# Two fused layers on one core: VectorE's first step on a gate tile moved next to its second step

## The chip, the cores and the metric

The kernel runs on one core of one Trainium2 chip. The metric is the device time of one execution in microseconds (us); the time of a version is the median of its runs. TensorE (PE in the rows) multiplies, its weight loads are PEld; VectorE is DVE, ScalarE is ACT, GpSimd is POOL, and SyncE (SP) issues most transfers.

## The reference

Two transformer layers on 2048 tokens of width 256, each of the form `x + attention(layernorm(x)) + ffn(layernorm(x))`. The first layer has linear attention and an FFN with ternary weights, and this FFN is where the change lies:

```python
def _L0_ffn_ref(x, W_up, W_gate, W_down):
    wu = ternary_quant(W_up)
    wg = ternary_quant(W_gate)
    wd = ternary_quant(W_down)
    up = jnp.einsum('bsd,ed->bse', x, wu)
    gate = jnp.einsum('bsd,ed->bse', x, wg)
    hidden = jax.nn.silu(up) * gate
    return jnp.einsum('bse,de->bsd', hidden, wd)
...
xn = _layernorm(x, axis=-1)
x = x + _L0_attn_ref(xn, ...) + _L0_ffn_ref(xn, ...)
xn = _layernorm(x, axis=-1)
x = x + _L1_attn_ref(xn, ...) + _L1_ffn_ref(xn, ...)
```

The second layer has softmax attention with rotary positions and an FFN with Hadamard-rotated weights.

## The kernel before, in words

`work_order()` writes one list of pieces (`gate`, `up`, `down`, `kv_in`, `att_n` and so on). Each engine walks this same list and, for every piece whose name it has a function for, issues its own instructions of that piece. So the list fixes the order of each engine's queue; engines meet only at semaphores. An engine that waits in one piece holds back everything behind it in its own queue.

The first layer's FFN goes over four chunks c of 512 tokens and, in each, over eight tiles m of 128 hidden units; f = 8c + m numbers them, and `gate 2` below means the gate piece of f = 2. TensorE forms the activated product in `gate` (line 938, four matmuls with the weights TU) and the other one in `up` (line 951, four with TG). Three tiles later `down` (line 917, weights TD) adds the tile's share of the output. Between these pieces `weave` puts pieces of the first layer's attention (`kv_in`, `kv_sum`, `att_n`, `att_t`, `att_b`, `q0`) and of the preparation of weights (`tern_cut`, `scales`, `spread_vb`, `butterfly`).

For the first two chunks (c below WHOLE = 2) silu is built from tanh, since exp of the attention is in the same table as tanh. The chain of one tile f is:

- TensorE `gate` writes a PSUM bank; ScalarE writes tanh of half of it to the buffer sg (line 1495, semaphore t);
- VectorE's first step: sg = (sg + 1) times the gate bank (line 1258, semaphore v1). This reads the gate bank for the last time;
- TensorE `up` writes another bank; VectorE's second step: sg = sg times the up bank (line 1267, semaphore h);
- ScalarE copies sg to hh (line 1503), GpSimd makes the rest hl (line 1633), and TensorE's `down` takes both.

From the third chunk on ScalarE applies Silu itself, and there is no first step on VectorE.

The gate and up products take their PSUM banks from one ring of three, banks 3, 4 and 5, in the order gate, up, gate, up. So `up` of tile f + 1 gets the bank of `gate` of tile f and waits, before its first matmul, for that tile's v1 (line 941); `gate` of tile f + 2 gets the bank of `up` of tile f and waits for h. The side pieces have banks 0 and 1: `att_n` (line 849) waits for the bank that the last `att_n` or `kv_in` left, which VectorE frees at line 1238 (`at`, the attention output divided by its sum) or line 1207.

VectorE's side pieces in the stretch at issue: `tern_cut` (line 1177) makes the ternary weights TD, 1024 columns at a time; `kv_in` is lines 1206 and 1207; `kv_sum` line 1226; `scales` lines 1193 to 1197; `spread_vb` line 1181; `att_n` lines 1232, 1234 and 1238; `att_t` line 1245; `att_b` line 1250.

Of the kernel before, what the change touches and what calls it, by code (L numbers as in the profile page):

```python
# [8 lines left out]
ALU = mybir.AluOpType  # L9
# [12 lines left out]
WHOLE = 2  # L22
# [422 lines left out]
def program(nc, x_d, wa0, tern, wa1, wo1, wf1, cols_d, bkv_d, cos_d, sin_d, had_d, mask_d, ident_d, pad_d, sel_d, wl_d, ob_d, wsd_d, y_d):  # L445
    with ExitStack() as ctx:
        base = -(-nc.sbuf_base // 32) * 32

        def sb(name, kb, shape, dt=F32):
            return nc.alloc_sbuf_tensor_at(name, shape, dt, offset=base + int(kb * KB))  # L450

        q = {n: ctx.enter_context(nc.semaphore(f"s_{n}")) for n in SEMAPHORES}
# [46 lines left out]
        sg = [sb(f"sg{i}", 168 + 2 * i, [128, 512]) for i in range(3)]  # L499
# [37 lines left out]
        bank = [PS[:, i, :] for i in range(8)]  # L537
# [56 lines left out]
        def way_out(e, p):  # L594
            (s_o, n_o), (s_n, _), (s_r, _), _ = o_slots(p)
            i, o = p // 4 % 2, p % 2
            e.dma_start(scr_o[p].rearrange("c k n -> (c k) n"), OE[o][:, :]).then_inc(d[s_o], 16)
            e.wait_ge(d[s_o], n_o)
            if p > 1:
                t, n = o_slots(p - 2)[3]  # L600
                e.wait_ge(d[t], n)
            e.dma_start(RC[o][:, :], scr_o[p, :, 16, :].rearrange("c (q n) -> c q n", n=16)).then_inc(d[s_r], 16)
            if p > 7:
                e.wait_ge(q["gl"], p // 4 - 1)
            for h in range(2):
                row = 32 * (p % 4) + 16 * h
                e.dma_start(NUM[i][row:row + 16, :].rearrange("r (a n) -> r a n", a=2),
                            scr_o[p, 2 * h:2 * h + 2, 0:16, :].rearrange("a r n -> r a n")).then_inc(d[s_n], 16)

        def recip_out(e, p):  # L610
            _, (s_n, _), _, (s_s, n_s) = o_slots(p)
            i = p // 4 % 2
            e.wait_ge(q["rcp"], p + 1)
            e.dma_start(scr_r[p].rearrange("c (q n) -> (c q) n", n=16), RC[p % 2][:, :]).then_inc(d[s_s], 16)
            e.wait_ge(d[s_s], n_s)
            for h in range(2):
                row = 32 * (p % 4) + 16 * h
                e.dma_start(DEN[i][row:row + 16, :].rearrange("r (a n) -> r a n", a=2),
                            scr_r[p, 2 * h:2 * h + 2, :].rearrange("(o a) n -> o a n", o=1).broadcast_to([16, 2, 512])).then_inc(d[s_n], 16)
# [472 lines left out]

        @block.vector
        def _(e):
            newest = {}

            def x_ready(c, m):

# [152 lines left out]
                newest[c, m] = q["xa"], 2 * c + m + 1  # L1251

            def gate(layer, c, m, b):
                f = 32 * layer + 8 * c + m
                s = sg[f % 3]
                if layer == 0 and c < WHOLE:
                    e.wait_ge(q["t"], f + 1)
                    e.scalar_tensor_tensor(s[:, :], s[:, :], 1.0, bank[b], ALU.add, ALU.mult).then_inc(q["v1"], 1)

            def up(layer, c, m, b):  # L1260
                if layer:
                    return
                f = 8 * c + m
                s = sg[f % 3]
                e.wait_ge(q["u"], f + 1)
                e.wait_ge(*(q["v1"], f + 1) if c < WHOLE else (q["t"], f + 1))
                e.tensor_tensor(s[:, :], s[:, :], bank[b], ALU.mult).then_inc(q["h"], 1)  # L1267

            def ffn_end(layer, c):
# [100 lines left out]
            def last(banks):  # L1370
# [14 lines left out]
                for i in range(2):  # L1385
                    for cc in range(2):
# [3 lines left out]

            parts = {f.__name__: f for f in (start, ln_stats, ln_norm, ln_turn, bias, w0l, signs, tern_scale, tern_cut, spread_vb, add_vb, half, scales, kv_in, kv_sums, q0,
                                             kv_sum, att_n, att_t, att_b, gate, up, ffn_end, prep_down, prep_ug, qk, qk_split, max_half, max_join, recip, join, project, last)}
            parts["max"] = max_tile
            for name, *args in order:
# [397 lines left out]
```

## Time and profile before

| | us |
|---|---|
| median of 3 runs | 740.97 (739.71 to 741.88) |
| the profiled execution | 741.94 |
| its span, first to last instruction | 740.0 |

The span is what the trace covers; 1.94 us of the profiled execution lie around it. The first layer's FFN with its first two chunks takes the stretch from 56 to 146 us of the span, chunks three and four follow until 229 us, and the second layer's softmax attention fills most of the rest. In the rows, a bracket at the end of a row is the time in which the engine was idle before that instruction, and what released it.

### The profile page before, as it was taken

Reading aid. Unit: us, or ns where it says so; the run is one execution under the profiler, and the core shown is the slowest. Engines: PE = TensorE matmul, PEld = TensorE weight load, DVE = VectorE, ACT = ScalarE, POOL = GpSimd, SP = SyncE. Lnnn points to the kernel's source line nnn. Section 1 sums busy time; section 2 is a strip of 40 time slices with the busy share of each in tenths; the row PEclk is TensorE's granted clock in tenths of the full one; section 3 lists DMA queues with packets and bytes.
Section 4 is the critical chain, followed back from the end, with each engine's and each line's share of the span. In section 5 each row is a group of like instructions: output and inputs, shape, how many; then the busy total and the mean of one; then the engine's idle time right before and its main releaser. Section 6 shows DMA issues by size and latency. Waiting matters only on the chain.

```text
span 740.0 us, 10943 instructions
## 1 busy us (share of the span) xinstructions
PE 696.3 (94%) x4186; PEld 437.3 (59%) x4186; DVE 524.2 (71%) x856; ACT 438.6 (59%) x600; POOL 295.8 (40%) x269
## 2 busy tenths in 40 slices
PE   3788899989999899999999998999999999999998
PEld 3576798977787778677677673333333333333345
DVE  4877866555578366678788878888897288888315
ACT  2454334446544532432432336999998899999883
POOL 1118846347657843542543431122224223333410
PEclk7799999999999999999999998999999999999999
DMA  6127101003024553423110112244444244423321
GB/s 260 57 77 279 58 0 58 1 2 115 0 86 152 182 166 98 140 90 115 57 58 2 57 58 76 80 144 151 139 138 149 93 147 141 157 90 94 102 81 58
DMA packets 25847, 74.13 MB, mean 100 GB/s; under 512 B 4620, under 2 KB 5996, under 8 KB 24964
## 3 DMA queue, kind: packets, MB, share of 16 engines
q1 hardware_dynamic: 21268, 65.37, 26.4%
q0 software_dynamic: 3808, 7.60, 3.5%
q8 instruction: 33, 0.54, 0.3%
q10 hardware_dynamic: 720, 0.48, 0.2%
q14 instruction: 18, 0.15, 0.1%
HBM read 54.54 MB, written 23.06 MB: 105 GB/s over the span
## 4 chain that ended last, share of the span: by engine, by line
PE 62%; POOL 2%; DVE 2%; ACT 1%; issue 1%; DMA 1%; SPq 0%; DVEq 0%; POOLq 0%; ACTq 0%
PE PS L1029 17%; PE PS L767 12%; PE PS L1015 12%; PE PS L773 9%; PE PS L998 6%; PE PS L988 5%; DVE mx L1329 1%; POOL sg L1642 1%; ACT P L1541 1%; DMA scr_k<-spl 1%; POOL rot L1663 1%; POOL rot L1662 1%; PE PS L1004 0%; ACT spl L1523 0%; ACT us L1506 0%
## 5 line engine op out<-in xcount | busy, mean ns | idle before, releaser
L1541 ACT ACTIVATE P<-PS 128x1024 f32<-128x1024 f32 x256 | 249.2, 1023 | 31.9 <-PE PS L1015 31.6
L1336 DVE TENSOR_REDUCE mx<-PS 128x1 f32<-128x512 f32 x300 | 189.2, 683 | 34.3 <-PE PS L998 32.7
L1329 DVE TENSOR_REDUCE mx<-PS 128x2 f32<-128x1024 f32 x106 | 124.8, 1221 | 37.4 <-PE PS L988 37.0
L1029 PE MATMUL PS<-P,VV 128*32 128x512 f32 x1024 | 137.6, 609 | 0.1
L1633 POOL TENSOR_TENSOR hl<-sg,hh 128x512 fp32r<-128x512 f32 x64 | 85.2, 1332 | 116.7 <-ACT hh L1511 67.4
L1015 PEld LDWEIGHTS PS<-QS,KS 64*128 64x128 f32 x512 | 48.9, 185 | 124.3 <-ACT P L1541 111.2
L1015 PE MATMUL PS<-QS,KS 64*128 64x512 f32 x512 | 117.7, 459 | 2.3 <-DVE mx L1329 1.8
L998 PE MATMUL PS<-KM,QM 64*128 64x512 f32 x300 | 82.0, 401 | 0.0
L1497 ACT ACTIVATE sg<-PS,cols 128x512 f32<-128x512 f32 x32 | 22.0, 688 | 82.1 <-PE PS L767 82.1
L1642 POOL TENSOR_TENSOR sg<-sg,us 128x512 f32<-128x512 f32 x32 | 42.1, 1316 | 37.5 <-ACT us L1506 37.5
L767 PE MATMUL PS<-XH,UGH 128*128 128x512 f32 x128 | 54.2, 423 | 1.6 <-ACT sg L1497 0.8
L767 PE MATMUL PS<-XL,UGH 128*128 128x512 f32 x128 | 50.5, 395 | 0.0
L767 PE MATMUL PS<-XH,UGL 128*128 128x512 f32 x128 | 50.0, 390 | 0.0
L1503 ACT ACTIVATE hh<-sg 128x512 fp32r<-128x512 f32 x32 | 20.1, 630 | 49.1 <-DVE sg L1267 49.1
L1029 PEld LDWEIGHTS PS<-P,VV 128*32 128x32 f32 x1024 | 20.3, 108 | 39.9 <-issue 34.4
L998 PEld LDWEIGHTS PS<-KM,QM 64*128 64x128 f32 x300 | 38.6, 188 | 3.5 <-DVE mx L1336 0.4
L988 PE MATMUL PS<-KM,QM 64*128 64x512 f32 x212 | 39.9, 448 | 0.8 <-DVE mx L1329 0.6
L773 PE MATMUL PS<-DH,hh 128*128 128x256 f32 x128 | 38.0, 297 | 0.0
L1506 ACT ACTIVATE us<-PS,cols 128x512 f32<-128x512 f32 x32 | 22.0, 687 | 25.6 <-PE PS L767 25.6
L773 PE MATMUL PS<-DL,hh 128*128 128x256 f32 x128 | 36.1, 282 | 0.0
L773 PE MATMUL PS<-DH,hl 128*128 128x256 f32 x128 | 36.1, 282 | 0.0
L773 PE MATMUL PS<-TD,hh 128*128 128x256 f32 x128 | 34.0, 300 | 1.6 <-POOL hl L1633 1.6
(211 smaller groups left out, 1346.6 us busy)
## 6 DMA issues: line engine op xcount, KB each, us to landing
QM<-scr_q SPq DMA_DIRECT2D x16, 512.0 KB, 4.4
KM<-scr_k SPq DMA_DIRECT2D x16, 512.0 KB, 5.3
QS<-scr_q SPq DMA_DIRECT2D x16, 512.0 KB, 4.3
KS<-scr_k SPq DMA_DIRECT2D x16, 512.0 KB, 5.2
scr_q<-spl SPq DMA_DIRECT2D x24, 256.0 KB, 3.3
scr_k<-spl SPq DMA_DIRECT2D x24, 256.0 KB, 3.4
scr_o<-OE POOLq DMA_DIRECT2D x14, 256.0 KB, 2.7
stg<-in_tern SPq DMA_DIRECT2D x3, 1024.0 KB, 4.8
```

The lines of the kernel that those rows point to most:

```text
L767: i = e.matmul(out, l, r, start=start and j == 0, stop=stop and j == len(pairs) - 1)
L773: i = e.matmul(out[:, r * 256:r * 256 + 256], l, x, start=first and r == 0 and j == 0, stop=last and j == len(pairs) - 1, skip_group_check ...
L988: e.matmul(bank[b + h], QM[p % 2][hr, qt * 128:(qt + 1) * 128], KM[p % 2][hr, chunk(half)], start=True, stop=True).then_inc(q["mt"], 1)
L998: e.matmul(bank[b], QM[p % 2][hr, qt * 128:(qt + 1) * 128], KM[p % 2][hr, chunk(half)], start=True, stop=True).then_inc(q["mt"], 1)
L1015: i = e.matmul(bank[b + h], KS[p % 2][hr, kt * 128:(kt + 1) * 128], QS[p % 2][hr, chunk(half)], start=True, stop=True)
L1029: i = e.matmul(PS[32 * c:32 * c + 32, 7, :], v_head(8 * b + kt, 2 * j + c // 2), P[s % 4][:, chunk(c // 2 + 2 * (c % 2))], start=(kt == 0) ...
L1329: e.tensor_reduce(mx[p % 2][:, :, qt, half], PS[:, b:b + 2, :], AX.X, ALU.max).then_inc(q["mx"], 2)
L1336: e.tensor_reduce(mx[p % 2][:, h, qt, half:half + 1], bank[b], AX.X, ALU.max).then_inc(q["mx"], 1)
L1497: e.activation(s[:, :], bank[b], ACT.Silu, scale=col("wsg", m) if layer else su).then_inc(q["t"], 1)
L1541: e.activation(P[s % 4][:, half * 1024:(half + 1) * 1024], PS[:, b:b + 2, :].rearrange("p b n -> p (b n)"), ACT.Exp).then_inc(q["ex"], 1)
L1633: e.tensor_tensor(hl[f % 4][:, :], sg[f % 3][:, :], r32(hh[f % 4][:, :]), ALU.subtract).then_inc(q["hl"], 1)
L1642: e.tensor_tensor(s[:, :], s[:, :], us[f % 4][:, :], ALU.mult).then_inc(q["h"], 1)
```

## The change

VectorE's first step on a gate tile is no longer issued at the place of `gate` in the list, but at the place of `up`, directly ahead of the second step. It waits for tanh (t) as before; the second step then waits for v1 and for the up product (u). `gates` remembers the bank. For chunks three and four only the order of two waits changes.

```diff
         @block.vector
         def _(e):
-            newest = {}
+            newest, gates = {}, {}
...
             def gate(layer, c, m, b):
-                f = 32 * layer + 8 * c + m
-                s = sg[f % 3]
-                if layer == 0 and c < WHOLE:
-                    e.wait_ge(q["t"], f + 1)
-                    e.scalar_tensor_tensor(s[:, :], s[:, :], 1.0, bank[b], ALU.add, ALU.mult).then_inc(q["v1"], 1)
+                gates[layer, c, m] = b
 
             def up(layer, c, m, b):
+
                 if layer:
                     return
                 f = 8 * c + m
                 s = sg[f % 3]
+                e.wait_ge(q["t"], f + 1)
+                if c < WHOLE:
+                    e.scalar_tensor_tensor(s[:, :], s[:, :], 1.0, bank[gates[layer, c, m]], ALU.add, ALU.mult).then_inc(q["v1"], 1)
+                    e.wait_ge(q["v1"], f + 1)
                 e.wait_ge(q["u"], f + 1)
-                e.wait_ge(*(q["v1"], f + 1) if c < WHOLE else (q["t"], f + 1))
                 e.tensor_tensor(s[:, :], s[:, :], bank[b], ALU.mult).then_inc(q["h"], 1)
```

Only VectorE's queue differs; those of TensorE, ScalarE, GpSimd and SyncE are the same row for row. The first step is line 1258 before and line 1264 after; the second is line 1267 in both.

VectorE around `gate 2`; sg_118, sg_119 and sg_120 are the buffers of tiles 0, 1 and 2 (and of 3, 4 and 5):

```order
 L1167 TENSOR_SCALAR s_53<-s_53 128x1
 L1169 TENSOR_SCALAR TD<-stg_122,s_53 128x2048
+L1264 SCALAR_TENSOR_TENSOR sg_119<-sg_119,PS 128x512
 L1267 TENSOR_TENSOR sg_119<-sg_119,PS 128x512
 L1245 TENSOR_TENSOR AL<-PS,AH 128x2x256
 L1177 SCALAR_TENSOR_TENSOR TD<-stg_122,s_53,TD 128x1024
-L1258 SCALAR_TENSOR_TENSOR sg_120<-sg_120,PS 128x512
 L1206 TENSOR_TENSOR zk_81<-PS,BKV 128x256
 L1207 TENSOR_TENSOR ve_89<-PS,BKV 128x2x128
```

Tile 1's first step now stands behind the long TD comparison, and tile 2's has left its place behind the first `tern_cut`.

VectorE around `up 2` and `up 3`, where tile 2's step comes back and tile 3's moves:

```order
 L1197 TENSOR_SCALAR s_53<-s_53 128x1
 L1181 TENSOR_SCALAR VBB<-ONES,cols 128x128 x2
-L1267 TENSOR_TENSOR sg_120<-sg_120,PS 128x512
-L1258 SCALAR_TENSOR_TENSOR sg_118<-sg_118,PS 128x512
+L1264 SCALAR_TENSOR_TENSOR sg_120<-sg_120,PS 128x512
+L1267 TENSOR_TENSOR sg_120<-sg_120,PS 128x512
 L1232 TENSOR_SCALAR rz_136<-PS 128x16
 L1234 RECIPROCAL rz_136<-rz_136 128x16
 L1238 TENSOR_TENSOR at_97<-PS,rz_136 128x256
+L1264 SCALAR_TENSOR_TENSOR sg_118<-sg_118,PS 128x512
 L1267 TENSOR_TENSOR sg_118<-sg_118,PS 128x512
```

Tile 2's first step now comes after `kv_in`, `kv_sum`, the second `tern_cut`, `scales` and `spread_vb`; the three rows of `att_n` no longer stand behind tile 3's first step.

## Rows read from the trace of the kernel before

**Rows 1.** The page's busy time of each engine over the span
```profile
PE 696.3 (94%) x4186; PEld 437.3 (59%) x4186; DVE 524.2 (71%) x856; ACT 438.6 (59%) x600; POOL 295.8 (40%) x269
```
**Rows 2.** Windows: PE, PEld, DVE, ACT, POOL busy (instructions), PE clock, DMA share, GB/s
```profile
60.00:80.00 20.00, 14.18 (x75) 11.26 (x74) 16.31 (x35) 7.10 (x13) 16.17 (x8) 1.00 0.64 214
80.00:100.00 20.00, 20.00 (x127) 18.00 (x126) 16.97 (x29) 8.71 (x17) 17.49 (x11) 1.00 0.01 1
```
**Rows 3.** Waits of VectorE, 56 to 145 us: total, times, longest
```profile
DVE sg L1258 <- ACT sg L1495: 9.9, 11, 1.4
```
**Rows 4.** Timeline of TensorE, 68 to 78 us: start, duration, instruction, idle before
```profile
68.33 0.73 PE L849 MATMUL PS<-kvb,QP 128*128 128x136 f32 x4 [0.65 <-DVE AL L1245]
...
71.01 0.50 PE L767 MATMUL PS<-XH,TG 128*128 128x512 f32 x1 [1.95 <-DVE sg L1258]
...
74.31 0.28 PE L773 MATMUL PS<-TD,hl 128*128 128x256 f32 x1
77.43 0.73 PE L849 MATMUL PS<-kvb,QP 128*128 128x136 f32 x4 [2.85 <-DVE at L1238]
77.91 0.48 PE L767 MATMUL PS<-XH,TU 128*128 128x512 f32 x1
```
**Rows 5.** Timeline of VectorE, 58 to 79 us
```profile
58.71 0.69 DVE L1258 SCALAR_TENSOR_TENSOR sg<-sg,PS 128x512 f32<-128x512 f32 x1 [0.99 <-ACT sg L1495]
59.51 0.69 DVE L1267 TENSOR_TENSOR sg<-sg,PS 128x512 f32<-128x512 f32 x1
...
68.19 2.17 DVE L1177 SCALAR_TENSOR_TENSOR TD<-stg,s,TD 128x1024 fp32r<-128x1024 f32 x1
70.28 0.67 DVE L1258 SCALAR_TENSOR_TENSOR sg<-sg,PS 128x512 f32<-128x512 f32 x1
70.88 0.41 DVE L1206 TENSOR_TENSOR zk<-PS,BKV 128x256 f32<-128x256 f32 x1
...
71.55 0.41 DVE L1226 SCALAR_TENSOR_TENSOR zk<-zk,ek 128x256 f32<-128x256 f32 x1
71.88 1.27 DVE L1177 SCALAR_TENSOR_TENSOR TD<-stg,s,TD 128x1024 fp32r<-128x1024 f32 x1
...
73.91 0.68 DVE L1267 TENSOR_TENSOR sg<-sg,PS 128x512 f32<-128x512 f32 x1
75.86 0.69 DVE L1258 SCALAR_TENSOR_TENSOR sg<-sg,PS 128x512 f32<-128x512 f32 x1 [1.27 <-ACT sg L1495]
...
76.95 0.42 DVE L1238 TENSOR_TENSOR at<-PS,rz 128x256 f32<-128x256 f32 x1
...
77.89 0.68 DVE L1250 TENSOR_TENSOR X<-PS,X 128x512 f32<-128x512 f32 x1
```
**Rows 6.** Timelines of GpSimd and VectorE where both read SBUF twice
```profile
68.01 3.48 POOL L1633 TENSOR_TENSOR hl<-sg,hh 128x512 fp32r<-128x512 f32 x2
81.10 1.31 POOL L1633 TENSOR_TENSOR hl<-sg,hh 128x512 fp32r<-128x512 f32 x1
81.18 1.50 DVE L1226 SCALAR_TENSOR_TENSOR zk<-zk,ek 128x256 f32<-128x256 f32 x1
```
**Rows 7.** Timelines of VectorE and TensorE at tiles 5 and 6
```profile
86.34 2.51 DVE L1226 SCALAR_TENSOR_TENSOR zk<-zk,ek 128x256 f32<-128x256 f32 x1
88.77 0.68 DVE L1267 TENSOR_TENSOR sg<-sg,PS 128x512 f32<-128x512 f32 x1
90.06 0.39 PE L767 MATMUL PS<-XH,TG 128*128 128x512 f32 x1
```
**Rows 8.** TensorE's clock around idle time: one timeline row, then windows
```profile
31.57 0.72 PE L767 MATMUL PS<-W0H,XH 128*128 128x512 f32 x1 [4.00 <-DVE ve L1207]
31.50:35.00 3.50, 3.43 (x10) 2.77 (x11) 3.29 (x11) 0.55 (x2) 0.44 (x1) 0.53 0.00 0
156.00:161.40 5.40, 2.76 (x17) 1.65 (x16) 2.67 (x8) 4.67 (x9) 3.18 (x2) 1.00 0.01 3
161.40:164.80 3.40, 3.40 (x15) 3.21 (x15) 1.04 (x2) 0.00 (x0) 1.69 (x2) 0.50 0.00 0
```

## The prediction, made before the changed kernel was run

> **What bounds the kernel now.** I read the page's engine shares first, then the windows of the stretch that the change touches, then its waits, and last the timelines of TensorE and VectorE side by side. TensorE is busy for 94% of the span [rows 1], so the question for any change elsewhere is whether it makes TensorE idle or takes idle time from it. The windows answer where that can be: from 60 to 80 us TensorE works 14.18 us of 20, from 80 to 100 us it works all 20 [rows 2]. In the first window it waits for VectorE, in the second VectorE has room (16.97 of 20 busy) and is not waited for. So the effect of the change is decided at tiles 1 to 3, and after that it is a matter of margins.
>
> The list of waits shows what the old place of the first step costs VectorE: it stood idle 9.9 us, 11 times, at most 1.4 us, for tanh [rows 3]. Behind it in the queue stood attention pieces that could have run. The new place lets them. What it takes away is the early release of the gate bank, on which `up` of the next tile waits. The timelines show both sides. TensorE waits 1.95 us at 71.01 for tile 2's first step, and 2.85 us at 77.43 for `at` [rows 4]. Before the latter VectorE had waited 1.27 us for tile 3's tanh and made the first step at 75.86, with the `at` chain behind it [rows 5].
>
> **The change part by part, in the order of the queue.** The step itself costs the same in both places. A 128x512 step is followed by the next instruction after 0.60 us where nothing connects them (70.28 to 70.88), and after 0.80 us where the second waits for the first (58.71 to 59.51) [rows 5]. Three of the 16 tiles (0, 6 and 11) had the two steps adjacent already, so 13 gaps of 0.20 us are new, 2.6 us of VectorE's time. Spread over 90 us, nearly all of it lies where VectorE has room, and I cost it at nothing on the path; if VectorE had no room, up to 2.6 us would show. The Trainium skill, page "VectorE: DVE Perf Modes", section "The DRAIN you can't avoid", says that a semaphore between two instructions costs nothing extra; by it these 2.6 us would be 0. The 0.80 against 0.60 of this trace speaks against that here.
>
> Tile 1: its step goes behind the TD comparison. The second step, and with it `up 2`'s release, comes about 0.2 us later. That delay is absorbed at once: the next `tern_cut` was issued at 68.19 but took 2.17 us where its twin at 71.88 took 1.27 [rows 5], because GpSimd was at work on hl from 68.01 [rows 6]. Issued 0.2 us later, it ends at the same time, 70.36.
>
> Tile 2 is the one that counts. Its first step leaves 70.28, and what stood behind it moves up by 0.60 us, until `kv_sum` (71.55, now 70.95). That reads SBUF twice. The same instruction at 81.18 took 1.50 us while GpSimd's hl ran from 81.10 to 82.41, so it ended 0.27 us after GpSimd [rows 6]. GpSimd's two hl end at 71.49, so here it ends at about 71.77 where it ended at 71.96 before. So only 0.2 of the 0.6 us is gained. The second `tern_cut`, `scales` and `spread_vb` follow as before, and the place of the old second step, 73.91, comes at 73.7. There the first step now stands; it ends 0.67 us later, and TensorE follows 0.06 us behind (70.95 to 71.01) [rows 4, 5]. So `up 3` starts at about 74.45 and not at 71.01: **3.4 us later**.
>
> What follows on TensorE is `up 3`, `att_b 0`, `down 0`, and then `att_n 3`, which waits for `at`. From 71.01 to the last of these matmuls at 74.31, and 0.12 us for it to be through, are 3.42 us [rows 4]. From 74.45 this reaches 77.87. The `at` that `att_n 3` waits for is no longer behind tile 3's tanh. VectorE's second step of tile 2 comes at 74.5, the `at` chain 0.60 us later, and it takes the 0.91 us that it took from 76.46 (that is 75.86 plus 0.60) to 77.37 [rows 5]. So `at` is there at 76.0 and `att_n 3` does not wait at all. **The 2.85 us wait goes, and a longer one at `up 3` takes its place**: `att_n 3` starts at 77.87 where it started at 77.43. With 0.1 us saved because matmuls run on without a pause, this is +0.4 us. I bound it at 0 (no hold by GpSimd, `kv_sum` as short as before) and +1.0 us (the second `tern_cut` held as its twin was, 2.17 against 1.27). The next side bank, freed by the addition at 77.89 [rows 5], comes no later, since that addition waited for VectorE and not for `att_b`.
>
> The clock is the second term. Before, TensorE's idle time around here was in two pieces of 1.95 and 2.85 us with 3.4 us of work between them [rows 4], and the granted clock stayed at 1.00 [rows 2]. Now it is one piece: the last work ends at 69.06 (68.33 plus 0.73) and the next starts at 74.45, 5.4 us. The nearest row is the wait of 4.00 us ahead of 31.57, and behind it the clock was 0.53 in the window from 31.5 to 35 us. After a stretch in which TensorE worked 2.76 us of 5.40 it was 0.50 for 3.4 us [rows 8]. So I expect one fall to 1.2 GHz, for 3.4 us or twice that. Each such 3.4 us that is all work loses half, 1.7 us; one that lies in the wait loses nothing. The term lies between 0 and 3.4 us. I take **+1.0 us**, between nothing and one full stretch, because part of the low time will lie inside the wait. The Trainium skill, page "TensorE: Matmul & The Clock Gate", section on the clock gate, says of the low clock that it is the default and that "activity releases the throttle"; by that too a longer idle piece speaks against this change, and the row of 4.00 us agrees.
>
> From `att_n 3` on TensorE is saturated. A shift of its queue there is passed on to the end, as each later wait depends on products of TensorE itself. The sum is 0.4 + 1.0 = **+1.4 us**. Against the profiled execution this is 741.94 + 1.4 = 743.3; that execution lies 0.97 above the median of the runs, so the forecast for the median is 740.97 + 1.4 = **742.4 us**, by itself 741.0 to 744.4 (0 and +3.4).
>
> **Rivals.**
>
> *The clock stays up.* The 1.95 and 2.85 us waits did not lower it, and it may also fall in executions of the kernel before, where this profile doesn't show it. Then only the 0.4 us is left: 741.4 us. Against it stands the 4.00 us row.
>
> *VectorE's backlog reaches TensorE (slower).* The place is `up 6`, which takes the bank of `gate 5`. Tile 5's first step now stands behind the `kv_sum` that was issued at 86.34 and held by GpSimd for 2.51 us, with the second step at 88.77 [rows 7]. The first step would take that place and end at 89.45; `up 6` started at 90.06, 90.5 with the shift. The margin is 1.0 us. GpSimd's own queue shifts too, since it waits for hh of tile 2. If `kv_sum` is held by one more GpSimd instruction there, it comes up to 2.1 us later (2.51 less the 0.41 that the row at 71.55 took alone [rows 5]), and TensorE stands for 1.1 us of it. Tile 8's bank for `up 9` is a second place of this kind. Two such give 740.97 + 1.4 + 2.2 = 744.6 us, and a third would give 745.7. For it: GpSimd is busy 17.49 of 20 us there [rows 2]. Against it: a low clock delays TensorE and widens these very margins, and a hold of the full length is a matter of luck.
>
> *VectorE's filled idle time wins (faster).* If VectorE's 9.9 us of waiting [rows 3] were on the path, taking the `at` chain out from behind tanh would gain what TensorE waited for it, 2.85 us, and a `tern_cut` that runs earlier could keep `up 3`'s extra wait below that. With 2.85 gained and nothing given back the time is 738.1 us. Against it stands the order of the queue: `up 3` cannot start before the place of 73.7.
>
> **How the numbers follow.** Forecast 0.55, clock stays 0.22, backlog 0.15, faster 0.08. A difference of 0.3%, 2.2 us, is about what a measurement of this kernel can tell from no change, and its limits are 738.75 and 743.2. Of the forecast, whose upper bound is 744.4, about a fifth lies above 743.2; with most of the backlog case that makes slower 0.23. Of the faster case three quarters lie below 738.75, 0.06. Within 0.3% is 0.71. The range takes in the forecast's own bounds, the clock case, half of each outer case, and the 1 us by which runs of this kernel lie apart: 739.9 to 744.8 us.
>
> **What the changed profile would show.** Right: a wait of about 5.4 us on TensorE at `up 3`, released by line 1264 of VectorE near 74.4, and no wait at the next line 849, which starts near 78 us or, with a low clock, up to 1.7 us later. VectorE's waits for tanh, 9.9 us before, shrink to a few us. From 80 to 100 us TensorE is busy for 20 of 20. A window of about 3.4 us with clock 0.50 starts between 72 and 78 us. Wrong: waits on line 1264 at tiles 6 or 9 (backlog), clock 1.00 throughout (clock stays), or `up 3` before 73 us (my reading of the queue). The whole estimate fails if the time moves by more than 4 us, as then something outside this stretch has changed.

## The result, and the profile of the changed kernel

| | before | changed |
|---|---|---|
| median, us | 740.92 (739.39 to 742.01, 20 runs) | 743.09 (738.86 to 743.98, 20 runs) |
| the profiled execution, us | 741.94 | 742.99 |
| its span, us | 740.0 | 740.9 |

The ratio is 1.0027, with a 95% interval of 1.0016 to 1.0037: slower by 2.2 us, which is just within 0.3%. The forecast of 742.4 us had 1.4 us of loss in it, so 0.7 us are missing. The two profiled executions differ by only 1.05 us, because the one of before lies 1.0 us above its median.

First the page's busy times and the windows of the changed kernel (same columns as [rows 2]), with one more stretch.

```profile
PE 696.0 (94%) x4186; PEld 437.6 (59%) x4186; DVE 523.7 (71%) x856; ACT 438.2 (59%) x600; POOL 294.7 (40%) x269
```
```profile
60.00:80.00 20.00, 13.59 (x68) 10.96 (x68) 16.26 (x31) 5.94 (x12) 15.63 (x7) 0.91 0.49 165
80.00:100.00 20.00, 20.00 (x123) 17.84 (x122) 14.28 (x30) 8.49 (x17) 15.96 (x9) 1.00 0.00 1
73.30:76.70 3.40, 2.89 (x9) 2.50 (x10) 2.82 (x7) 1.21 (x2) 1.48 (x2) 0.50 0.85 300
```

No engine's busy time moved by more than 1.1 us against [rows 1]. From 60 to 80 us TensorE lost 0.59 us of work against [rows 2] and its mean clock fell from 1.00 to 0.91; from 80 to 100 us it still works all 20. The third window shows the low clock: it starts at 73.3 us and lasts 3.4 us.

TensorE's timeline of the changed kernel, 65 to 79 us, which answers to [rows 4]:

```profile
65.81 0.50 PE L767 MATMUL PS<-XH,TG 128*128 128x512 f32 x1 [1.26 <-DVE sg L1264]
...
68.41 0.73 PE L849 MATMUL PS<-kvb,QP 128*128 128x136 f32 x4 [0.48 <-DVE AL L1245]
...
73.81 0.79 PE L767 MATMUL PS<-XH,TG 128*128 128x512 f32 x1 [4.67 <-DVE sg L1264]
...
78.53 0.63 PE L849 MATMUL PS<-kvb,QP 128*128 128x136 f32 x4
```

`up 3` waits 4.67 us where it waited 1.95, and `att_n 3`, the last row, does not wait at all where it waited 2.85. From the start of `up 3` to `att_n 3` 4.72 us pass; before, the same work was through in 3.42 [rows 4]. The 1.30 us between are the low clock: the first matmul of `up 3` takes 0.79 us where it took 0.50.

VectorE's timeline of the changed kernel, which answers to [rows 5] and, in its last rows, to [rows 7]:

```profile
58.08 0.69 DVE L1264 SCALAR_TENSOR_TENSOR sg<-sg,PS 128x512 f32<-128x512 f32 x1 [0.98 <-ACT sg L1495]
58.80 0.69 DVE L1267 TENSOR_TENSOR sg<-sg,PS 128x512 f32<-128x512 f32 x1
...
61.82 3.34 DVE L1169 TENSOR_SCALAR TD<-stg,s 128x2048 fp32r<-128x2048 f32 x1
65.08 0.67 DVE L1264 SCALAR_TENSOR_TENSOR sg<-sg,PS 128x512 f32<-128x512 f32 x1
...
68.27 1.45 DVE L1177 SCALAR_TENSOR_TENSOR TD<-stg,s,TD 128x1024 fp32r<-128x1024 f32 x1
69.64 0.41 DVE L1206 TENSOR_TENSOR zk<-PS,BKV 128x256 f32<-128x256 f32 x1
70.31 0.82 DVE L1226 SCALAR_TENSOR_TENSOR zk<-zk,ek 128x256 f32<-128x256 f32 x1
71.05 1.27 DVE L1177 SCALAR_TENSOR_TENSOR TD<-stg,s,TD 128x1024 fp32r<-128x1024 f32 x1
...
73.08 0.68 DVE L1264 SCALAR_TENSOR_TENSOR sg<-sg,PS 128x512 f32<-128x512 f32 x1
73.79 0.69 DVE L1267 TENSOR_TENSOR sg<-sg,PS 128x512 f32<-128x512 f32 x1
...
74.89 0.42 DVE L1238 TENSOR_TENSOR at<-PS,rz 128x256 f32<-128x256 f32 x1
75.75 0.69 DVE L1264 SCALAR_TENSOR_TENSOR sg<-sg,PS 128x512 f32<-128x512 f32 x1 [0.44 <-ACT sg L1495]
...
86.77 1.97 DVE L1226 SCALAR_TENSOR_TENSOR zk<-zk,ek 128x256 f32<-128x256 f32 x1
88.66 0.68 DVE L1264 SCALAR_TENSOR_TENSOR sg<-sg,PS 128x512 f32<-128x512 f32 x1
```

Tile 2's first step now stands at 73.08, behind everything that the order shows ahead of it, and `up 3` follows 0.05 us after its end. `at`, the attention output that `att_n 3` used to wait for, is there at 75.31 (74.89 plus 0.42), more than 3 us before `att_n 3`. Two adjacent steps start 0.72 us apart (58.08 to 58.80), where they were 0.80 apart before and 0.60 apart when nothing connects them.

The list of VectorE's and TensorE's waits in the changed kernel, 56 to 145 us, which answers to [rows 3]:

```profile
DVE AL L1245 <- ACT AH L1462: 8.6, 6, 1.9
...
PE PS L767 <- DVE sg L1264: 5.9, 2, 4.7
...
DVE sg L1264 <- ACT sg L1495: 2.8, 4, 1.0
```

VectorE's waits for tanh shrank from 9.9 us in 11 to 2.8 us in 4, and bought almost nothing: TensorE had waited for what stood behind them only once, at `att_n 3`. TensorE waited for line 1264 twice, at tile 1 and at tile 2, and never after that.

**Shifts.** To place gains and losses I lay TensorE's matmuls of two profiles over each other in order and subtract their start times; the difference, positive where the other profile is later than that of before, is called the shift. The changed kernel is 0.66 us ahead at 59 us, before any moved step can matter. That has nothing to do with the change: the profile of before has a low clock from 41.9 to 45.3 us and the changed one has not, and of the profiles below, those with such a stretch at 41 us (e1, e5, e6, e11) are within 0.2 us of before at 59 us, and the others 0.3 to 0.8 ahead. Then from 59 to 79 us the shift goes from −0.66 to +1.01: **1.67 us are lost in the stretch of the prediction**, and after that it stays at about +0.8 to +1.2 to the end. So the table below gives only what the shift changes inside a stretch.

| kernel | low clock, start (length) in 65 to 85 us | change of shift, 59 to 79 us | 150 to 172 us |
|---|---|---|---|
| changed | 73.3 (3.4) | +1.67 | 0.0 |
| e5, changed again | 72.3 (6.8) | +2.42 | +0.1 |
| e2, tile 2 alone | 71.4 (6.8) | +2.26 | +0.1 |
| e1 and e6, fillers | none | +0.42, +0.39 | +1.35, +1.27 |
| e3, all but tile 2 | none | −0.88 | +1.35 |
| e7, all but tiles 1 and 2 | 69.9 (6.8) | −0.34 | +0.90 |
| e11, tile 3 alone | 72.0 (3.4) | −0.92 | +0.1 |
| e8, tile 3 behind the addition | 70.9 (3.4) | −1.62 | 0.0 |
| e4, fillers in before | none | −0.04 | 0.0 |
| e10, fillers at 158 in before | 71.5 (3.4) | −0.07 | −1.51 |
| e9, fillers in both places | none | +0.35 | −1.46 |

### The profile page after: what moved, and what is told of

The parts are those of the page before. It is cut to its first block, busy times and chain, and to the rows that moved or that the text cites. A ratio compares the mean times of both kernels' runs of the same rounds, so it can differ in the third digit from the quotient of the medians.

```text
span 740.9 us, 10943 instructions
## 1 busy us (share of the span) xinstructions
PE 696.0 (94%) x4186; PEld 437.6 (59%) x4186; DVE 523.7 (71%) x856; ACT 438.2 (59%) x600; POOL 294.7 (40%) x269
## 4 chain that ended last, share of the span: by engine, by line
PE 61%; POOL 2%; DVE 2%; ACT 1%; issue 1%; DMA 1%; SPq 0%; DVEq 0%; POOLq 0%; ACTq 0%
PE PS L1029 17%; PE PS L767 12%; PE PS L1015 12%; PE PS L773 9%; PE PS L998 6%; PE PS L988 5%; DVE mx L1329 1%; POOL sg L1642 1%; ACT P L1541 1%; DMA scr_k<-spl 1%; POOL rot L1662 1%; POOL rot L1663 1%; PE PS L1004 0%; ACT spl L1523 0%; ACT us L1506 0%
```

## The experiments

My theory was that of the prediction: tile 2's step delays `up 3` (queue), and the merged idle time lowers the clock (clock). Rivals were that the fall of the clock happens in before as well and costs nothing extra, that the 0.2 us gaps or tile 1 carry the loss, and that TensorE is no bound where I say it is. All runs were timed beside the kernel before; its medians were 740.98 (21 runs, for e1 to e4), 740.78 (29, for e5 to e8) and 740.91 us (33, for e9 to e12).

**e1_fill_after and e6_fill_again: the changed kernel with TensorE kept busy ahead of `up 3`.** The fillers write bank 2, which nobody reads; all the kernel's own work is done.

```diff
+            def filler(n):
+                e.wait_ge(q["kvs"], 1)
+                for _ in range(n):
+                    e.matmul(bank[2], TU[:, 0, 0:128], XH[:, 0, 0:512], start=True, stop=True)
...
                 f = 32 * layer + 8 * c + m
+                if f == 3:
+                    filler(16)
```

> The changed kernel, with 16 matmuls more of 128x512 on TensorE ahead of `up 3`, into PSUM bank 2, which nobody uses then; at 0.23 us each they take 3.7 us of the 4.67 us for which TensorE waits there. Theory (the loss is a later `up 3` plus one low-clock stretch): `up 3` starts at the same time as in the changed kernel, the clock stays at 1.00 around 73 to 77 us, and the time falls by the 1.3 us that the low clock cost, to about 0.7 us (0.1%) over the kernel before. Rival (the low clock costs nothing, because the work behind it waits anyway, and the loss is VectorE's): no change against the changed kernel, still 2 us (0.27%) over the kernel before. Rival (more work on TensorE costs time): slower than the changed kernel by up to 3.7 us.

> The changed kernel with 16 matmuls more ahead of `up 3`, once more. The first time `att_n 3` came 0.7 us earlier than in the changed kernel's profile and the clock stayed up there, but the median was no lower. Theory (the low clock costs 1.3 us, and the first median was high by chance): 0.5 to 1.5 us below the changed kernel beside it. Rival (what the clock leaves at 73 us is lost again further down, where TensorE waits at 158 to 162 us or at 255 us for other engines and the clock falls anyway): within 0.4 us of the changed kernel beside it.

Measured: 743.36 us (742.52 to 745.21, 5 runs, ratio 1.0035, 1.0021 to 1.0049) and 742.95 us (739.85 to 743.76, 12 runs, 1.0023, 1.0007 to 1.0040). Against the kernel before the loss stays almost whole. Against the changed kernel timed beside it (e5, 743.72 us) e6 is 0.8 us lower, inside its theory's 0.5 to 1.5, but their intervals overlap, and e1 is no lower than the changed kernel's 743.09. As a cure it failed. The profiles say why. `up 3` in e1's TensorE timeline, and then the windows of e1 and of e6 around the next idle time:

```profile
74.40 0.50 PE L767 MATMUL PS<-XH,TG 128*128 128x512 f32 x1 [1.05 <-DVE sg L1271]
```
```profile
155.00:170.00 15.00, 12.32 (x61) 10.34 (x60) 7.18 (x17) 6.42 (x13) 5.51 (x5) 0.77 0.11 29
```
```profile
60.00:80.00 20.00, 17.26 (x90) 13.83 (x89) 17.05 (x34) 6.74 (x13) 15.61 (x8) 1.00 0.64 218
155.00:170.00 15.00, 12.32 (x62) 10.38 (x61) 6.99 (x17) 6.49 (x14) 5.66 (x4) 0.77 0.10 25
```

The clock stays at 1.00 around `up 3`, and the queue term stands alone: +0.42 and +0.39 us in the table. So the rest of the changed kernel's +1.67 is the clock: 1.25 us. But at 161 us, where before and both profiles of the changed kernel have one low stretch of 3.4 us, the filled one has 6.8, and loses 1.3 us there. It is not the filling as such: e3, e7 and e12, which have no filler, have 6.8 us there too. The low clock began 0.7 to 0.8 us before TensorE took up work again (161.0 against 161.8 in e6), while before it began 0.2 us after (161.4 against 161.2). Whether that idle time costs one low stretch or two seems to be decided by a small shift of the time line; no run shows more than that the two go together.

**e2_tile2_only and e3_tile2_old: the part of tile 2.** e2 is the kernel before with only tile 2's step moved; e3 is the changed kernel with only tile 2's step at its old place. `first` issues the first step; in `gate` it is called where the step keeps its old place. e3, against the changed kernel (in e2 both conditions are turned round, so that tile 2 alone moves; in e2, e3, e7 and e11 the second step's two waits stand in the new order for all tiles):

```diff
                 gates[layer, c, m] = b
+                f = 32 * layer + 8 * c + m
+                if layer == 0 and c < WHOLE and not (f != 2):
+                    first(f, b)
...
                 if c < WHOLE:
-                    e.scalar_tensor_tensor(s[:, :], s[:, :], 1.0, bank[gates[layer, c, m]], ALU.add, ALU.mult).then_inc(q["v1"], 1)
+                    if f != 2:
+                        first(f, gates[layer, c, m])
                     e.wait_ge(q["v1"], f + 1)
```

> The kernel before, with only tile 2's first step moved behind the place of its `up`. Theory (tile 2 alone decides): a wait of about 4.5 to 5 us at `up 3`, a low clock behind it, and a time 1.5 to 2.2 us over the kernel before, as the whole change. Rival (the loss comes from the 13 tiles whose steps are now adjacent, or from tile 1): within 0.3 us of the kernel before.

> The changed kernel, but tile 2's first step back at the place of `gate`. Theory (tile 2 alone decides, and tile 3's step gives a gain that it hid): `up 3` starts near 71 us after a wait of 1 to 2 us, `att_n 3` does not wait for VectorE's `at`, the next wait is at `kv_in 10` for the addition of `att_b 0`, and the time is 0.5 to 1.5 us below the kernel before. Rival (the loss comes from the other tiles): 1 to 2 us over the kernel before, as the changed kernel.

Measured: e2 743.23 us (742.52 to 744.45, 5 runs, 1.0032, 1.0019 to 1.0044), e3 739.69 us (739.07 to 740.27, 11 runs, 0.9988, 0.9977 to 0.9999). TensorE's timelines, first of e2, then of e3:

```profile
73.84 0.80 PE L767 MATMUL PS<-XH,TG 128*128 128x512 f32 x1 [5.40 <-DVE sg L1262]
```
```profile
70.35 0.50 PE L767 MATMUL PS<-XH,TG 128*128 128x512 f32 x1 [1.25 <-DVE sg L1262]
...
74.81 0.73 PE L849 MATMUL PS<-kvb,QP 128*128 128x136 f32 x4 [0.89 <-DVE at L1238]
...
77.26 0.50 PE L767 MATMUL PS<-W0H,XH 128*128 128x512 f32 x1 [0.80 <-DVE X L1250]
```

Tile 2 alone reproduces the whole loss, wait and low clock included. Without it, the other twelve moved steps are not a loss but 1.3 us of gain: `att_n 3` waits 0.89 instead of 2.85 us. Loss and gain do not add (2.25 less 1.3 is 1.0, and the whole change costs 2.2): once `up 3` is late, `att_n 3` does not wait in e2 either, and there is nothing left to be gained at it. In e2, where tile 1 stays in its old place, the wait is the forecast 5.40 us; in the changed kernel it is 4.67, because tile 1's delay moved the work ahead of it.

**e4_fill_before: does TensorE's idle time in the kernel before cost anything by itself?** The same filler, 6 ahead of `up 3` and 9 ahead of `att_n 3`.

> The kernel before, with 6 matmuls more ahead of `up 3` (1.4 us of its 1.95 us wait) and 9 ahead of `att_n 3` (2.1 us of its 2.85 us wait). Theory (in the kernel before, too, the clock falls here in some executions, which the one profile does not show): up to 1 us faster than the kernel before in the median. Rival (its clock never falls here): within 0.3 us of the kernel before.

Measured: 741.23 us (11 runs, 1.0003, 0.9994 to 1.0012), clock 1.00 from 60 to 80 us and a change of shift of −0.04. Filling these waits is worth nothing. It is also the control for e1: 15 added matmuls cost nothing.

**e5_after_again: the changed kernel once more**, since 1.05 and 2.17 us of the first profiles and medians did not agree.

> The changed kernel once more, as the base for the three kernels that run beside it on the same chip. Every theory: 1.5 to 2.5 us (0.2 to 0.34%) over the kernel before, `up 3` after a wait of 4.5 to 5.5 us.

Measured: 743.72 us (742.78 to 745.3, 6 runs, 1.0046, 1.0029 to 1.0063), 2.9 us over before and so above the expected 1.5 to 2.5. This profile lies on that of before up to 59 us (shift −0.02), so it can be read against [rows 4] directly. TensorE's timeline and the window of the low clock:

```profile
66.44 0.50 PE L767 MATMUL PS<-XH,TG 128*128 128x512 f32 x1 [1.19 <-DVE sg L1264]
...
74.45 0.80 PE L767 MATMUL PS<-XH,TG 128*128 128x512 f32 x1 [4.68 <-DVE sg L1264]
```
```profile
72.30:79.10 6.80, 4.65 (x18) 4.27 (x19) 4.85 (x13) 1.84 (x3) 3.25 (x2) 0.50 0.44 157
```

`up 3` starts at 74.45, the predicted time to the hundredth. But here the low clock lasts for 6.8 us, `att_n 3` starts at 79.93 (5.48 us after `up 3`, 2.06 of them clock), and the stretch costs 2.42 us. One and the same program has either one or two low stretches here. From 80 to 100 us this profile loses another 0.6 us (the shift goes from 2.38 to 2.96): the weight loads of `att_n` wait for VectorE in two places.

```profile
88.82 0.53 PEld L849 LDWEIGHTS PS<-kvb,QP 128*128 128x128 f32 x4 [0.21 <-DVE AL L1245]
93.82 0.53 PEld L849 LDWEIGHTS PS<-kvb,QP 128*128 128x128 f32 x4 [0.48 <-DVE at L1238]
```

Neither wait is in the first profile of the changed kernel.

**e7_tiles12_old: does tile 1 lose something of its own?** As e3, but with `f not in (1, 2)` for `f != 2`: tiles 1 and 2 keep their old places. `up 2` had waited 1.26 us for tile 1's step in the changed kernel, a rival to tile 2.

> The changed kernel with the first steps of tiles 1 and 2 back at the place of `gate`. Theory (tile 2 carries the loss, tile 1 only a wait of 1.2 us at `up 2` that a later hold absorbs): no wait at `up 2`, and the time is that of the kernel with tile 2 alone put back, 1.3 us below the kernel before, within 0.4 us. Rival (the 1.2 us at `up 2` is a loss of its own): 1 us or more below the kernel with tile 2 alone put back, that is 2 to 2.5 us below the kernel before.

Measured: 740.28 us (739.42 to 740.74, 12 runs, 0.9997, 0.9986 to 1.0007). That is 0.6 us above e3 and not below it, so tile 1 in its new place is no loss, though the theory's "within 0.4 us" of e3 is missed too. Its profile puts 0.5 us of the 0.6 in this stretch (−0.34 against e3's −0.88): there it has 6.8 us of low clock from 69.9, where e3 has none, and `att_n 3` starts without a wait. Whether its other runs have the same I do not know.

**e11_tile3_only: where the gain is.** The kernel before with only tile 3's step moved (`f == 3`).

> The kernel before, with only tile 3's first step moved behind the place of its `up`. Theory (the gain of the change is in tile 3 alone, as `att_n 2` no longer stands behind tanh): a wait of 1.9 us at `up 3`, none or under 1 us at `att_n 3`, one at `kv_in 10` for the addition, and 0.5 to 1.3 us below the kernel before, as with tile 2 alone put back. Rival (the gain of that kernel came from other tiles): within 0.3 us of the kernel before.

Measured: 739.57 us (739.02 to 740.12, 11 runs, 0.9979, 0.9971 to 0.9988). All of e3's gain is in tile 3. `up 3` stays at 71.00 with its 1.95 us wait, and `att_n 3`, freed from tile 3's tanh, starts at 75.93 without a wait instead of at 77.43.

**e8_tile3_after_add: further in the same direction.** The kernel before with both steps of tile 3 behind the addition of `att_b 0`.

```diff
                 newest[c, m] = q["xa"], 2 * c + m + 1
+                if (c, m) == (0, 0):
+                    s = sg[0]
+                    e.wait_ge(q["t"], 4)
+                    e.scalar_tensor_tensor(s[:, :], s[:, :], 1.0, bank[5], ALU.add, ALU.mult).then_inc(q["v1"], 1)
...
                 s = sg[f % 3]
+                if f == 3:
+                    late.append(b)
+                    return
```

> The kernel before, with both steps of tile 3 moved behind `att_n 2` and the addition of `att_b 0`; all other tiles as before. Theory (VectorE's idle time ahead of tile 3's step, and then the addition behind it, is what TensorE waits for at 77 us): `att_n 3` starts at about 74.8 us instead of 77.43, `kv_in 10` waits no longer for the addition, the queue gains 2 to 2.9 us there, and the time falls by 1.5 to 2.9 us below the kernel before. Rival (work that comes earlier is given back at the next wait on another engine, at 125 or 158 us): less than 0.7 us below the kernel before.

Measured: 738.96 us (735.5 to 740.13, 12 runs, 0.9978, 0.9963 to 0.9992), 1.8 us faster than before and 4.8 us faster than the changed kernel timed beside it (e5): it beats both. `att_n 3` starts at 75.27, and the stretch gains 1.62 us although a low clock of 3.4 us lies in it.

**e9_fill_both and e10_fill158_before: the price of a low stretch.** e9 is e1's kernel with 9 more fillers at 158 to 162 us, in the layer norm of step 4 and ahead of `att_b` of chunk four; e10 is the kernel before with those 9 alone.

```diff
                 for t in range(4):
+                    if n == 4 and t % 2 == 0:
+                        filler(2, 2)
...
             def att_b(c, m, b):
+                if (c, m) == (3, 0):
+                    filler(5, 2)
```

> The changed kernel with fillers in two places: 16 matmuls ahead of `up 3`, as before, and 2, 2 and 5 more in the three waits of 0.7, 0.6 and 1.3 us around the second layer's first layer norm (158 to 162 us). The fill ahead of `up 3` alone gave 0.7 us at 77 us of the trace less than it should keep: behind 161 us the clock was low for 6.8 us instead of 3.4. Theory (the low clock is what is lost, and it moved from 73 to 161 us): no low clock from 46 to 250 us, the shift against the kernel before stays at 0.4 to 0.6 us less about 1.6 us for the low stretch that the kernel before has at 161 us, and the time is 0.5 to 1.5 us below the kernel before. Rival (the clock's cost is hidden at 161 us, as other engines are waited for anyway): no better than the fill ahead of `up 3` alone, 1.7 to 2.5 us over the kernel before.

> The kernel before with the fillers at 158 to 162 us alone. It measures the price of one low stretch by itself: TensorE is saturated behind it, so the full 3.4 us at half clock should show. Theory: the clock stays at 1.00 at 161 us and the time falls by 1.3 to 1.7 us (0.2%) below the kernel before. Rival (the clock falls later instead, at 179 or 211 us, or the gain is lost at 255 us): within 0.5 us of the kernel before.

Measured: e9 739.38 us (737.99 to 742.37, 12 runs, 0.9991, 0.9975 to 1.0007), e10 738.72 us (737.44 to 742.37, 12 runs, 0.9974, 0.9963 to 0.9985). The windows of e10, to be read against the last of [rows 8]:

```profile
155.00:170.00 15.00, 14.30 (x91) 12.05 (x90) 8.63 (x25) 8.89 (x16) 8.14 (x6) 1.00 0.20 71
161.00:164.40 3.40, 3.40 (x23) 3.05 (x23) 1.45 (x4) 0.69 (x1) 1.30 (x2) 1.00 0.00 0
```

In the 3.4 us in which the kernel before works on 15 matmul instructions at clock 0.50, e10 works on 23 at 1.00, and its shift gains 1.51 us. e9 removes both low stretches, those at 73 and at 161 us, and is 3.6 us below e6, which removes the first only. In e9 and e10 the shift also gains 0.7 and 1.6 us between 245 and 276 us, far from any filler. In e10 the low clock of before at 260.4 us is missing there, which is worth as much; why it is missing I did not find out. So of e10's 2.2 us in the median, above the 1.3 to 1.7 expected, 1.5 are what its trace shows for the fillers.

Up to 155 us e10 is the kernel before, and its profile has a low stretch from 71.5 us that the profile of before has not. The window of that stretch, and TensorE's two waits around it:

```profile
71.50:74.90 3.40, 3.40 (x18) 3.40 (x17) 2.23 (x7) 1.07 (x2) 0.36 (x1) 0.50 0.37 125
```
```profile
70.23 0.50 PE L767 MATMUL PS<-XH,TG 128*128 128x512 f32 x1 [1.96 <-DVE sg L1267]
...
76.65 0.73 PE L851 MATMUL PS<-kvb,QP 128*128 128x136 f32 x4 [1.33 <-DVE at L1247]
```

TensorE works through all 3.4 us at half clock, and yet the stretch costs nothing (−0.07): the wait for `at` behind it is 1.33 us where it was 2.85. So the clock falls here with the old order too, in some executions, and the second wait takes up its cost. The changed kernel no longer has that wait, and pays.

**e12_tile3_scales: can `up 3`'s own wait be shortened as well?** e8 with `scales` and `spread_vb` moved behind `att_n 2` in VectorE's list.

> The best version so far (both steps of tile 3 behind the addition of `att_b 0`, 1.8 us below the kernel before), with `scales` and `spread_vb`, 0.84 us of VectorE, also moved, from ahead of tile 2's second step to behind `att_n 2`. Theory (VectorE's queue from 71.9 to 77.4 us is what `att_n 3` waits for): `at` is 0.8 us earlier; as TensorE's own path is then as long, 0 to 0.8 us below that version, so 1.8 to 2.6 us below the kernel before. Rival (TensorE's path or its clock is the limit already): the same as that version within 0.3 us.

Measured: 743.77 us (740.52 to 746.06, 10 runs, 1.0041, 1.0028 to 1.0054), 4.8 us slower than e8. Both theory and rival fell. VectorE's row of `spread_vb` in e8, then rows of GpSimd and VectorE, and TensorE's next wait, in e12:

```profile
72.85 0.47 DVE L1181 TENSOR_SCALAR VBB<-ONES,cols 128x128 f32<-128x128 f32 x2
```
```profile
75.10 4.52 POOL L1604 TENSOR_TENSOR stg<-stg,WSD 128x2048 f32<-128x2048 f32 x1
...
75.26 4.63 DVE L1181 TENSOR_SCALAR VBB<-ONES,cols 128x128 f32<-128x128 f32 x2
...
79.82 0.68 DVE L1250 TENSOR_TENSOR X<-PS,X 128x512 f32<-128x512 f32 x1
...
80.55 0.50 PE L767 MATMUL PS<-W0H,XH 128*128 128x512 f32 x1 [3.70 <-DVE X L1250]
```

A pair of instructions of 0.47 us took 4.63, because GpSimd's fold had begun just before: it ends at 79.62, the pair at 79.89. TensorE then stood 3.70 us and the clock fell again, at 81.0 us; the shift goes from −0.66 at 59 us to +3.31 at 81. The trace agrees with the Trainium skill, page "GPSIMD Engine Reference", section "8. Key points", that GpSimd shares its SBUF interfaces with VectorE; how long a hold lasts only the rows tell.

## Why the prediction was right, and where it was short

The time, 743.09 us, lies in the range, 0.7 us above the forecast; the likeliest case came about.

- **Queue, +0.4 us: right, and measured alone.** e1 and e6 give +0.42 and +0.39. The steps behind it held too: tile 2's first step at the old place of the second, `up 3` at 74.45 in e5, no wait at `att_n 3`, and the next side bank no later.
- **GpSimd's hold on `kv_sum`: right.** It was to end 0.27 us after hl. In the changed kernel hl ends at 70.84 (started at 67.36, 3.48 long, as in [rows 6]) and `kv_sum` at 71.13, 0.29 later.
- **Tile 1, "about 0.2 us later": wrong in size, right in effect.** In e5, aligned with before, `up 2` comes 0.75 us later. I had taken it that the long TD comparison would move forward by the 0.60 us that the first step gave up ahead of it. It was issued earlier, but it ended no earlier: GpSimd's additions to X hold it as they hold `kv_sum`. VectorE's comparison and GpSimd's next addition, before, and that addition in the changed kernel (its comparison is the row at 61.82):

```profile
63.17 2.63 DVE L1169 TENSOR_SCALAR TD<-stg,s 128x2048 fp32r<-128x2048 f32 x1
64.66 3.39 POOL L1588 TENSOR_TENSOR X<-X,OB 128x1024 f32<-128x1024 f32 x1
```
```profile
64.01 3.39 POOL L1588 TENSOR_TENSOR X<-X,OB 128x1024 f32<-128x1024 f32 x1
```

  The comparison ends at 65.80 before and at 65.16 in the changed kernel, 1.1 us after GpSimd has gone on to its next addition in both, and in e5 it was issued at 62.47 and ended at 65.79. So the whole first step, 0.7 us, was added behind it. The delay was absorbed as predicted, by the next `tern_cut`, which took 1.45 instead of 2.17 us: it too ends 1.1 us after GpSimd's first hl in both orders.
- **13 gaps of 0.20 us at no cost: right in the medians.** From 80 to 100 us TensorE has no idle time in the changed kernel's profile, e2 alone carries the whole loss and e3 has none. The gap is 0.12 us (0.72 against 0.60), not 0.20, with the waits in the new order.
- **Clock, +1.0 us: the term that was mis-sized.** Its place, its kind and a length of 3.4 us "or twice that" were right, its size was too small. I took 1.0 "because part of the low time will lie inside the wait". One stretch cost 1.25 to 1.30 us though it began 0.5 us before `up 3`, and two cost 2.06. With 0.4 that makes 1.7 to 2.4 us, and the medians showed 2.2 and 2.9. What I had not seen is why it costs anything: not that the clock falls only in the new order, but that no wait stands behind the low stretch any more to take it up (e10). The mean clocks of all runs do not show how often it falls. Seven of the fourteen profiles show a low stretch of 17.1 us near 8 us of the span and seven do not, though TensorE's eight matmuls from 8 to 16 us take 1.94 us in the profiles of before (shown clock 0.50) and of e10 (1.00) alike, so that record says nothing of the time. The profiles with it have mean clocks of 0.979 or less, those without 0.984 or more; taking the runs up to 0.981 to have it, they are 36 of the 83 runs of before and 18 of the 26 of the changed kernel. Without it the runs have an estimated 21.4 and 22.5 us of low clock, 1.1 us more in the changed kernel (standard error 0.9), which is less than one stretch.
- **The bounds were added up wrongly.** The forecast's own upper bound, +3.4 us, is that of the clock alone; with the queue's +1.0 it should have been +4.4, 745.4 us. The queue term's own rows give 0.44 less 0.1, rounded up to 0.4; that it hit 0.42 and 0.39 so closely is partly luck.
- **Rivals.** Backlog at `up 6` or `up 9` did not come: `kv_sum` was held for 1.97 us, tile 5's step began at 88.66 and TensorE did not wait. In e5, with two low stretches, VectorE's backlog did reach TensorE, at `att_n` and not where I had looked, for 0.6 us. The clock didn't stay up; that it also falls in the old order, which I had named there, is what e10 shows. The faster case had a true core that I valued too low: taking the `at` chain out from behind tile 3's tanh gains 1.3 us (e11); the change gave it away at tile 2.

What stays open: what share of the runs of either kernel has no, one or two low stretches here, and so how the 2.2 and 2.9 us of the medians divide between queue, clock and backlog (the 0.4 and 1.25 us are those of single profiles); and the shifts of 1 to 1.6 us near 260 us, which come and go between profiles (in e1 a GpSimd instruction there waited 2.76 us for a DMA and not 1.16).

## What to carry to other kernels

Before a step is moved within an engine's queue, list what stands between its old and its new place, and who waits for what it releases; a step that was early for one consumer may have been the release of another. Thirteen moved steps were here one loss, one gain and eleven that changed nothing in the medians, and moving the one alone gave 1.3 us. What is moved past work of an engine that shares memory interfaces is priced by that engine's timeline, not by the instruction's own duration (e12: 0.47 us became 4.63). And a wait on a matmul-bound engine is priced with the clock behind it: 4.67 us of idle time in one piece, where 4.80 had been in two, cost 1.25 us of clock beside 0.4 us of delay. The second of two waits had been the place where a low stretch cost nothing.

## What the runs showed of the hardware that I had not expected

- **The clock's price.** A low stretch of 3.4 us costs 1.25 to 1.5 us where TensorE has no wait behind it (changed kernel at 73 us, e10's gain at 161 us), and nothing where it has: in e10's own profile TensorE worked through one from 71.5 us, and the next wait was 1.5 us shorter. It is the slack behind it that counts. The Trainium skill, page "TensorE: Matmul & The Clock Gate", section "HAM oscillation — how this bites in real kernels", says that a wait between pieces of compute makes the engine start the next piece cold, and the 0.80 us of `up 3`'s first matmul in e5, against 0.50, agrees. In e10 the clock fell though the longest wait from 60 us on had been 1.96 us.
- **Where the low stretch falls changes between executions.** Two profiles of the same program have 3.4 and 6.8 us of it at the same place, and the filled kernel paid at 161 us what it had saved at 73.
- **Work that nobody reads made the kernel faster.** Nine matmuls in idle time at 158 to 162 us took 2.2 us off the kernel before (e10); the same kind of filler in the two waits at 71 and 77 us gave nothing (e4).
- **A hold by GpSimd ends with its running instruction, whenever VectorE's was issued.** From 40 to 150 us the profiles of before, of the changed kernel and of e5 have 14 `kv_sum` that took over 0.5 us, and all of them end 0.28 or 0.29 us after a GpSimd instruction; alone `kv_sum` takes 0.41. The pair of `spread_vb` in e12 ends 0.27 us after it. The larger ones take longer behind it: the TD comparison and the first `tern_cut` end 1.08 us after it, where their twins on TG take 1.29 and 1.28 us alone. GpSimd is held in turn: the addition to X beside the comparison took 3.39 us, and the median of its eight is 2.40.
